# Attention and mixture-of-experts layer on one core: expert tiles moved between the turns of attention

## The reference, cut to what matters

```python
xn = layernorm(x)                                   # [2048, 128]
q, k, v = (heads(xn @ W) * mod for W in (Wq, Wk, Wv))   # mod = cos(phase) * amplitude
scores = q @ k.T / sqrt(8) * cos(2 pi (i - j) / 2048)
w = softmax(scores)
w = (w + roll(w, 1, axis=-1)) / sqrt(2)
attn = (w @ v) @ Wo
# experts: top 2 of 8 by a small gating attention over xn @ wqkv.T
a, g = split(x_rep @ w1[e].T)                       # 2 x 352
y = (silu(a) * g) @ w2[e].T                         # back to 128
out = x + attn + sum of the two y, weighted by the gates
```

## Time and profile before

| what | value |
| --- | --- |
| time, median of 3 runs | 709.84 us (708.99 to 710.26) |
| the profiled execution, its time | 707.88 us |
| the profiled execution, its span | 706.1 us |
| PE busy | 621.4 us, 88% |
| ACT busy | 550.1 us, 78% |
| DVE busy | 220.7 us, 31% |
| POOL busy | 93.3 us, 13% |
| PE weight loads (beside PE) | 201.4 us, 29% |
| first exponential of attention | 207.76 us |
| last one ends | 690.8 us |

### The profile page before, as it was taken

One profiled execution on the slowest core, in us unless ns is written; L12 is line 12 of the kernel. 1 busy time (PEld: TensorE's weight loads), 2 busy tenths in 40 slices (PEclk: granted clock), 3 DMA queues, 4 the chain that ended last, 5 costly groups with the idle time before them and its releaser, 6 DMA issues.

```text
span 706.1 us, 11470 instructions
## 1 busy us (share of the span) xinstructions
PE 621.4 (88%) x4151; PEld 201.4 (29%) x4152; DVE 220.7 (31%) x462; ACT 550.1 (78%) x530; POOL 93.3 (13%) x109
## 2 busy tenths in 40 slices
PE   3984057999989999999999999999999999999995
PEld 3841034677751111111111111111111111111113
DVE  7578024334420031423233142331414232005003
ACT  1466024233358999999999999999999999999992
POOL 2038720111110101010010101101010000000000
PEclk9998568899998999999999999999999999999999
DMA  4934321111141101011010101101010010000002
GB/s 129 313 121 148 120 62 66 45 45 59 48 131 47 43 5 46 16 31 36 12 46 1 47 16 31 43 3 46 1 46 25 19 35 1 3 1 1 1 0 63
DMA packets 33828, 34.44 MB, mean 49 GB/s; under 512 B 6092, under 2 KB 27878, under 8 KB 33650
## 3 DMA queue, kind: packets, MB, share of 16 engines
q1 hardware_dynamic: 30786, 27.01, 13.3%
q0 software_dynamic: 2992, 6.76, 2.9%
HBM read 21.14 MB, written 12.58 MB: 48 GB/s over the span
## 4 chain that ended last, share of the span: by engine, by line
PE 60%; ACT 18%; issue 13%; DVE 7%; SPq 2%; DMA 0%; ACTq 0%; DVEq 0%
PE ps L1098 23%; ACT big L581 16%; PE ps L1081 15%; PE ps L981 4%; PE ps L974 4%; PE ps L986 3%; DVE m L771 2%; PE ps L964 2%; SPq L339 2%; PE ps L1116 2%; PE ps L1105 1%; PE ps L915 1%; PE ps L906 1%; DVE big L717 1%; PE ps L959 1%
## 5 line engine op out<-in xcount | busy, mean ns | idle before, releaser
L581 ACT ACTIVATE big<-ps 128x1536 f32<-128x1536 f32 x342 | 471.2, 1459 | 11.9 <-PE ps L1081 4.5
L1098 PE MATMUL ps<-big,vh 128*32 128x512 f32 x2048 | 274.1, 607 | 0.1
L1081 PE MATMUL ps<-qa,ka 49*128 49x512 f16 x896 | 179.8, 385 | 12.2 <-ACT big L581 9.2
L771 DVE TENSOR_REDUCE m<-ps 128x1 f32<-128x512 f32 x128 | 88.5, 692 | 157.5 <-PE ps L1116 157.5
L1081 PEld LDWEIGHTS ps<-qa,ka 49*128 49x128 f16 x896 | 33.1, 93 | 227.1 <-ACT big L581 157.1
L1098 PEld LDWEIGHTS ps<-big,vh 128*32 128x32 f32 x2048 | 40.4, 108 | 103.8 <-issue 98.2
L436 POOL COPY vh<-vaug 128x144 f32 x16 | 5.1, 319 | 382.1 <-PE ps L1098 380.8
L1116 PE MATMUL ps<-ka,attnT 49*128 49x512 f16 x128 | 48.0, 375 | 6.0 <-DVE m L771 5.7
L755 DVE COPY osb<-ps 128x512 f32<-128x512 f32 x16 | 11.1, 692 | 126.7 <-PE ps L1098 126.7
L738 DVE TENSOR_TENSOR cs<-pair,ps 128x352 f32<-128x352 f32 x39 | 20.3, 521 | 85.2 <-PE ps L986 81.6
L553 ACT COPY y<-ps 128x128 f32<-128x128 f32 x39 | 10.4, 266 | 45.6 <-PE ps L974 45.6
(11 more groups left out here) (165 smaller groups left out, 370.9 us busy)
## 6 DMA issues: line engine op xcount, KB each, us to landing
qk_parts<-store SPq DMA_DIRECT2D x16, 256.0 KB
qa<-qk_parts SPq DMA_DIRECT2D x28, 128.0 KB
slots_x<-vh SPq DMA_DIRECT2D x5, 512.0 KB, 9.1
cs<-slots_x SPq DMA_DIRECT2D x20, 128.0 KB, 2.3
slots_y<-y POOLq DMA_DIRECT2D x19, 128.0 KB, 2.7
store<-in_L_ffn_w SPq DMA_DIRECT2D x4, 512.0 KB, 6.6
ka<-qk_parts SPq DMA_DIRECT2D x32, 64.0 KB, 2.1
qa<-qk_parts SPq DMA_DIRECT2D x28, 64.0 KB
```

Source lines behind the costliest of these rows:

```text
L581: nc.scalar.activation(probs[:, first % PROBS:first % PROBS + n, :], ps[:, first % RING:first % RING + n, :], ACT.Exp, scale=ISQ8 / (OPERA ...
L771: nc.vector.tensor_reduce(m4[:, j // NC, j % NC:j % NC + 1], ps[:, O_BANKS[(p - 1) % 2], :], AX, ALU.max).then_inc(m_reduced, 1)
L1081: ins = nc.tensor.matmul(ps[:, n % RING, :], k[at:at + KQ, P * o:P * o + P], q[at:at + KQ, CW * c:CW * c + CW], start=True, stop=True, til ...
L1098: ins = nc.tensor.matmul(ps[32 * c:32 * c + 32, O_BANKS[p % 2], :], vh[:, p % 2, o + 8 * b, :], probs[:, n % PROBS, :], start=k == 0, stop ...
```

## The change

The stages are reordered, and the expert tiles are computed between the turns of attention.

- The query, key and value projections come straight behind the normalisation, then the head order, and attention begins. The first angle operations on DVE move ahead of the normalisation's end; their loads go to ACT's queue, and the memset of `ka` goes from DVE to POOL. The expert weights are loaded after the first two heads' operands. The values are projected between the query and key steps.
- The first 11 heads (704 score tiles) run in **pairs** of tiles in four banks (352 turns); banks 4 and 5 are free for the expert work. The other 320 tiles run in triples as before (107 turns).
- The gating products, the slot assignment (`RANK_TURN` 24), the 24 weight blocks (one in each turn from 26, now copied out by DVE) and from turn 70 the 39 expert tiles, seven turns each, are issued behind the scores and quads of their turn. POOL scatters once the slots are there.
- The expert tile is changed: step 0 transposes the rows; step 2 computes both halves of the first layer as six matmuls of 128 columns with the weights stationary, so that the hidden units lie on the partitions and need no transposition afterwards; after the exponential of step 3 ACT computes exp(-a) (`decay_of`), and DVE forms 1/(1 + exp(-a)), times a, times g in four operations (`hidden`) instead of one multiplication and one copy; step 6 is the second layer. Silu's table isn't used any more. PE takes the weights from one of four staging buffers, which SP fills for each tile with two DMAs inside the on-chip memory (`stage_weights`).
- The results are stored by SP, the gathers come one with each quad from quad 174. The maximum jobs start with head 3, 13 a head, and skip steps 4 and 5 of a tile. Of `xnT`, whose place the attention result takes, a copy is kept in DRAM for the rare second pass.

The diff, cut to its core:

```diff
+PAIRED = 11 * PER_HEAD
+PAIRS = PAIRED // 2
+PAIR_RING, PAIR_PROBS = 4, 16
+RING, PROBS = 2 * GROUP_OF, 5 * GROUP_OF
+SCORE_GROUPS = PAIRS + -(-(SCORE_TILES - PAIRED) // GROUP_OF)
...
+FIRST_JOB_HEAD = 3
+JOBS_A_HEAD = 13
 JOB_QUAD = 6
+MIX_BEFORE = 8
+MIX_AT = 1
+PAIR_EXP_AT = 12
+TOP_EXP_AT = 30
+RANK_TURN = 24
+WEIGHTS_AT = 26
+EXPERTS_AT = 70
+TURNS_A_TILE = 7
+GATHER_AT = 174
...
+        def expert_step(g):
+
+            m, step = divmod(g - EXPERTS_AT, TURNS_A_TILE)
+            return (m, step) if 0 <= m < TILES else (None, None)
+
+        def weight_block(g):
+
+            i = g - WEIGHTS_AT
+            return i if 0 <= i < E * NF else None
+
+        def turns():
+
+            w, j = 0, 0
+            for g in range(SCORE_GROUPS + 2):
+                m, step = expert_step(g)
+                job = None
+                if (w % QUADS >= JOB_QUAD and j < jobs_before(w // QUADS + 1) and step not in (4, 5)
+                        and (g < PAIRS or (g - j) % 2 == 0)):
+                    job = (w // QUADS, j)
+                    j += 1
+                ready = first_of(g - 1) if g >= 1 else 0
+                quads = range(w, max(w, min(ready // NC, H * QUADS)))
+                w = quads.stop
+                yield g, job, quads
 
         def run_again(eng):
...
+            def stage_weights(m):
+
+                if m == 0:
+                    sp.wait_ge(owner_ready, 1)
+                    sp.wait_ge(wT_ready, E * NF)
+                after(sp, y_ready, m - STAGES + 1)
+                e = sp.value_load(expert_of[0:1, m:m + 1], min_val=0, max_val=E - 1)
+                k = m % STAGES
+                sp.dma_start(w1_of[k], w1T[:, bass.ds(e, 1), :].rearrange("p o f -> p (o f)")).then_inc(staged_ld[k], 16)
+                sp.dma_start(w2_of[k], w2T[:, bass.ds(e, 1), :, :].rearrange("p o f h -> p (o f) h")).then_inc(staged_ld[k], 16)
+
...
+            for g, job, quads in turns():
+                m, step = expert_step(g)
+                for p in range(2, PLAIN):
+                    if g == groups_for(PER_HEAD * (p - 1)):
+                        sp.wait_ge(score_ready, g)
+                        load_head(p)
+                if g == EXPERTS_AT - 4:
+                    load_rows(0)
+                    load_rows(1)
+                    for first in range(STAGES - 1):
+                        stage_weights(first)
+                if g == EXPERTS_AT:
+                    sp.wait_ge(rows_ready, 2)
+                    for r in range(EXACT):
+                        load_operands(head_at(PLAIN + r), qe[:, r, :], ka[:, 2 + r, :], exact_ld)
+                if step == 1 and m + STAGES - 1 < TILES:
+                    stage_weights(m + STAGES - 1)
+                if step == 1 and m % 2 == 1 and m // 2 + 2 < ROW_PAIRS:
+                    load_rows(m // 2 + 2)
+                if step == 0 and m % 2 == 0 and m >= 2:
+                    store_results(m // 2 - 1)
+                if g == EXPERTS_AT + TURNS_A_TILE * TILES:
+                    store_results(ROW_PAIRS - 1)
...
+            def decay_of(m):
+
+                act.wait_ge(a_ready, m + 1)
+                after(act, hidT_ready, m - 1)
+                nc.scalar.activation(decay[:, m % 2, :], ps[:, 4, 0:FP], ACT.Exp, scale=-1.0).then_inc(decay_ready, 1)
...
+                if g == PAIR_EXP_AT:
+                    act.wait_ge(gexp_in, 1)
+                    nc.scalar.activation(pair[:], pair[:], ACT.Exp).then_inc(gexp_out, 1)
+                if g == TOP_EXP_AT:
+                    act.wait_ge(gexp_in, 2)
+                    nc.scalar.activation(top[:, 5, :], top[:, 4, :], ACT.Exp).then_inc(gexp_out, 1)
+                m, step = expert_step(g)
+                if step == 3:
+                    decay_of(m)
...
+            def rows_out(m):
+                dve.wait_ge(xgT_ps, m + 1)
+                after(dve, g_ready, m - 1)
+                nc.vector.tensor_copy(xgT[:, m % 2, :], ps[:, 4, FP:FP + P]).then_inc(xgT_ready, 1)
+
+            def hidden(m):
+
+                k = m % 2
+                dve.wait_ge(decay_ready, m + 1)
+                then(nc.vector.tensor_scalar(decay[:, k, :], decay[:, k, :], 1.0, BIGGEST, ALU.add, ALU.min))
+                then(nc.vector.reciprocal(decay[:, k, :], decay[:, k, :]))
+                dve.wait_ge(a_ready, m + 1)
+                then(nc.vector.tensor_tensor(decay[:, k, :], decay[:, k, :], ps[:, 4, 0:FP], ALU.mult))
+                dve.wait_ge(g_ready, m + 1)
+                after(dve, y_ready, m - 1)
+                nc.vector.tensor_tensor(hidT[:, k, :, :].rearrange("p f s -> p (f s)"), decay[:, k, :], ps[:, 5, 0:FP],
+                                        ALU.mult).then_inc(hidT_ready, 1)
+
+            def result_out(m):
+                dve.wait_ge(y_ready, m + 1)
+                after(dve, y_wr[m // 2 % 2], m // 4 * 16)
+                nc.vector.tensor_copy(y[:, m % 4, :], ps[:, 5, FP:FP + DM]).then_inc(y_copied, 1)
...
+            for g, job, quads in turns():
+                if job is not None:
+                    take_max(*job)
+                for w in quads:
+                    p, k = w // QUADS, w % QUADS
+                    if p >= 1 and k == 0:
+                        copy_out(p - 1)
+                    if p >= 1 and k == 2:
+                        normalise(p - 1)
+                    if jobs_before(p) < JOBS and jobs_before(p + 1) == JOBS and k == QUADS - 2:
+                        make_exact_shift(p)
+                    if p == PLAIN and k == JOB_QUAD:
+                        for j in range(2 * NT):
+                            add_result(j)
+                if g == RANK_TURN:
+                    assign_slots()
+                if g == EXPERTS_AT - 1:
+                    gates()
+                if weight_block(g) is not None:
+                    take_weights(weight_block(g))
+                m, step = expert_step(g)
+                if step == 0:
+                    rows_out(m)
+                if step == 3:
+                    hidden(m)
+                if step == 6:
+                    result_out(m)
             copy_out(H - 1)
             normalise(H - 1)
...
+            def turn_rows(m):
+
+                pe.wait_ge(xg_ld[m // 2 % 2], m // 4 * 16 + 16)
+                after(pe, xgT_ready, m)
+                if m == 0:
+                    pe.wait_ge(wT_ready, E * NF)
+                nc.tensor.transpose(ps[:, 4, FP:FP + P], xg[:, m % 4, :], ident[:]).then_inc(xgT_ps, 1)
...
+            def widen(m, b, ready):
+
+                pe.wait_ge(staged_ld[m % STAGES], (m // STAGES + 1) * 32)
+                pe.wait_ge(xgT_ready, m + 1)
+                after(pe, hidT_ready, m)
+                if b == 1:
+                    after(pe, y_copied, m)
+                for f, (f0, n) in enumerate(FCH):
+                    ins = nc.tensor.matmul(ps[0:n, 4 + b, P * f:P * f + P],
+                                           w1_of[m % STAGES][:, F * b + f0:F * b + f0 + n],
+                                           xgT[:, m % 2, :], start=True, stop=True)
+                ins.then_inc(ready, 1)
+
+            def result(m):
...
+            def expert_work(g):
+                m, step = expert_step(g)
+                if step == 0:
+                    turn_rows(m)
+                elif step == 2:
+                    widen(m, 0, a_ready)
+                    widen(m, 1, g_ready)
+                elif step == 6:
+                    result(m)
...
+                after(pe, exp_done, g if g == PAIRS else g - 1)
+                if g == PAIRS:
+                    pe.wait_ge(hidT_ready, TILES)
+                    pe.wait_ge(y_copied, TILES)
...
+            pe.wait_ge(rot_ready, 16)
+            pe.wait_ge(v_ready, 4)
+            for g, job, quads in turns():
                 if g < SCORE_GROUPS:
                     scores(g)
-                if w % QUADS >= JOB_QUAD and j < jobs_before(w // QUADS + 1) and (g - j) % 2 == 0:
-                    max_job(w // QUADS, j)
-                    j += 1
-                while w < H * QUADS and tiles_of_quad(w)[-1] < (g - 1) * GROUP_OF:
+                if job is not None:
+                    max_job(*job)
+                for w in quads:
                     weighted_values(w)
                     between(w)
-                    w += 1
+                if 0 <= g - MIX_AT < (NT - MIX_BEFORE) // 2:
+                    for t in range(2):
+                        mix_tokens(MIX_BEFORE + 2 * (g - MIX_AT) + t)
+                if g == RANK_TURN:
+                    rank_tokens()
+                if weight_block(g) is not None:
+                    turn_weights(weight_block(g))
...
```

More of the change, by code:

```diff
@@ L735, in turn_tile @@
[L735 to L740 removed]
+            dve.wait_ge(const_ld, 3 * 16)
+            dve.wait_ge(norm_parts, 4)
+            for g in range(2):
+                nc.vector.tensor_scalar(sel16[:, g, :], sel[:], square_sum[:, 2 * g + 1:2 * g + 2], 1.0 / S,
```

(28 more changed lines are left out.)

657 lines of the change are left out of this document (266 added, 391 removed).

## The result

The changed kernel takes 877.12 us (median of 4 runs, 871.34 to 880.73) against 709.84. The ratio is 1.235, with a 95% interval of 1.228 to 1.242. The forecast was 780 and the range ended at 850; the rival in which every stall costs the clock had 870. The profiled execution took 871.34 us, with a span of 869.5.

The account below looks back on a forecast made before the run. TensorE and ScalarE are near their limit in attention, and each tile becomes a serial chain: 60 + 81 + 413 + 24 + 8.3 + 144 + 15.3 + 31 = 777 us of span, forecast 780, range 715 to 850.

Parts of the forecast that it names:

- every stall costs the clock: Rival for the tiles: all 39 stalls pay 3.1 us of clock, 121 in place of 31, so 870 us; chance 0.15.
- The chain: Expert tile: TensorE waits at step 6 for VectorE's 4.09 us hidden gate, making the tile one serial chain.
- The alternation: Tiles take 10.1 us, or 11.1 every second tile with two quads ahead of the widening; 413 us in all.
- The jobs: Maximum jobs in paired turns, five to a tile in 21 tiles, add 24 us (0 to 30).
- The clock: After stalls TensorE runs at its lower clock: 1.55 us for each of the 20 longer stalls, 31 us.
- the earlier trace: Kernel before the change: clock low after 3.23 and 1.65 us idle, but not after 1.56.
- The start: Work that must still run before attention's first exponential: 60 us, allowed 53 to 70.
- the rest: After the tiles: nine turns 8.3 us, 107 triples 144, the end as now 15.3; copies and gathers nothing.
- The last triples: End of attention: 107 triples at 1.346 us each, 144 us.
- turns 0 to 69: Paired attention turns before the first tile, with weight blocks and row loads: 81 us, first tile near 141.
- Hidden chain short: Rival for the tiles: reciprocal at a copy's pace, 0.55 us, chain 79 us less, clock kept: 670 us; chance 0.12.

Follow-up runs that it names:

- e3: The changed kernel with the two score matmuls of step 6 issued nine times instead of once, same result; 790 us.
- e7: The changed kernel with decay and hidden at step 2, no job at step 3, and the second layer at step 0 of the next tile; 737 us.
- e2: The changed kernel with the reciprocal of the gate replaced by a multiplication with 0.5, so without the division; 711.6 us.
- e1: The changed kernel with the decay and the four operations of hidden issued at step 2 instead of step 3; 758 us.
- e10: The changed kernel with only ScalarE's decay moved to step 2 and the second layer to step 0 of the next tile; 763 us.
- e5: e1 with no maximum job at step 3; jobs may begin at quad 3 of a head instead of 6; 733 us.
- e15: e12 with VectorE's last two operations of hidden at step 6, behind a job's maximum, run on another chip; 717.8 us.
- e12: e10 with the second half of the first layer moved to step 3; 724 us.

## Why the prediction was right in direction and wrong in size

**The chain: right.** TensorE waits 39 times on the last product. The hidden gate was 4.09 us; measured 0.36 + 2.55 + 0.55 + 0.55 with the gaps, 305.09 to 309.21, 4.12. The reciprocal, from its slope, 2.57 for 2.55. For the scores of step 3 the chain has 0.42 without a row; the trace has 0.39. The stall was 2.5 in one half of the tiles and 2 or less in the other; measured 2.13 on average.

The Trainium skill (VectorE: DVE Perf Modes, "First, the fixed hardware budget") gives the reciprocal a repeat count of 8; read as 8 cycles a column that was an estimate of 3.2 us, and the trace does not agree: it has 2.55 us and, by the slope, 6 cycles at that page's 0.96 GHz.

**The alternation: right, its level 0.7 too low.** 10.1 and 11.1 us became 10.66 and 11.55 in e3's tiles without jobs, where the clock is out of it, and 11.28 on average with the turns of a head's end among them. Some 0.3 is the twelve and six matmuls with their weights: 1.52 us from start to next in e7's trace for the first layer (predicted 1.34), 0.77 for the second (0.67). The jobs come to (11.79 - 11.28) x 38 = 19 us; the forecast was 24.

**The clock: the step that failed.** "Bounds 0 to 3.1 a tile; I take the middle, 1.55, for the 20 longer stalls: 31 us." Measured: 87 us at least, 1.94 a tile on average and near 2.9 in tiles with five jobs, and the shorter stalls pay as well (1.64 us at 309.27, with the clock at 0.51 behind it). The mechanism was in the prediction; its size was not. With 87 in place of 31 the sum is 836, inside the range.

The argument for so small a term was the earlier trace rows, where the clock held after 1.56 us of idle time. That row is one stall, and one stall does not give a share: nine of the change's 39 have no spell behind them either, and 30 have. What decides between the two was not measured. It may be the other short waits near a stall, but the stretches do not show it plainly: TensorE works 4.08 us of the 6 around the stall at 309.27 (305 to 311), behind which the clock fell, and 4.39 of the 6 around that of the earlier trace rows (110.3 to 116.3), behind which it held.

The Trainium skill (TensorE: Matmul & The Clock Gate, "A second HAM failure mode: psum-queue depth-cycling") tells of frequent small idles that make the clock swing. The trace agrees, with 29 spells at the lower level in 528 us, and this described the case better than the row that I set against it.

**The start and the rest.** The first exponential came at 67.0 instead of 60 (within 53 to 70). The last triples took 149.4 us from 704.45 to 853.85 for 144. Summed against the span of 777: start 7, turns 0 to 69 about 3, tiles 39 x (13.73 - 12.0) = 67, of which the clock has 39 x (1.94 - 0.8) = 44 and the level of the chain 39 x (11.8 - 11.2) = 23, the stretch from the last tile to the triples 9, the triples 5. That is 91 of the 92.5. Of the 9 the clock has 6.8 as well, by e3: the spell of 20.5 us at its lower level covers that stretch. The prediction had no clock term there.

**The rivals.** "Every stall costs the clock" said 870, which is nearest to the measured 877, and had 0.15; it should have had the most. That it is so near is in part luck: it priced the clock at 121, and e3 gives 87 or a little more, in 30 spells for its 39 stalls; the level of the chain, the start and the rest made up the difference. Its 6.2 us a spell was right on average. "Hidden chain short" has a lesson of its own: with the chain made short (e2) the kernel reads 711.6 and not 670, because attention and tiles together leave TensorE little room. I had written that it has hardly any time to give away, and then took 79 us off without asking it.

## What to carry to other kernels

When work is put between the steps of a loop that keeps TensorE busy, price a stall by what TensorE does for the next several microseconds as well, not by its own length alone: here 83 us of stalls brought at least 87 us of loss by slower matmuls. Before an operation goes onto an engine's queue, list what is queued behind it and who waits for that; in three of the misses above (e1, e7, e10) TensorE stood for a reduction of 0.69 us queued behind a gate of 4.1. In e1 that was most of the miss by e5 (25 us), in e10 the merged step and its clock were more. And to hide work in a stage, add up its cost on the engine that is already near its limit: with most of the waits taken away (e2, e15) the kernel was still not below the kernel before.

## What the runs showed of the hardware

- Repeating matmuls whose result is already there made the kernel 10% faster (e3, 877 to 790 us), with the granted clock up from 0.80 to 0.85 to 1.00 and no work taken away.
- With one stall of 1.3 to 3.1 us in each tile of 11 to 17 us, and shorter waits beside it, the clock was at its lower level for 181 of 528 us, in 29 spells of 3 to 10 us. Stalls of 1.64 us stand both among those with a spell behind them and among those without. In e12 eight waits of 1.26 us left it mostly at 1.00 (0.97 to 1.00 in stretches of 100 us, two spells), in e10 sixteen of some 1.76 us did not (0.85 to 0.96, eleven spells); the two also differ in the merged step.
- RECIPROCAL on VectorE: 248 ns for 16 columns, 953 for 128, 2553 for 384, so 6.25 to 6.3 ns a column; a multiplication by a scalar of the same 384 columns takes 362.
- On one chip two programs began their tiles some 37 us late beside a scatter by GpSimd, while ScalarE and VectorE stood for up to 12 and 17 us at a time; one of them, run on another chip, did not. The cause is open.
